# One-hots and spline products of a graph network on one core: the second operand of VectorE in PSUM

## What is computed

```python
h = relu(layernorm(x)); x = x + L0(h, edge_index, edge_attr_2)    # two SplineConv layers, 25 weights
h = relu(layernorm(x)); x = x + L1(h, edge_index)                 # normalised neighbour sum
h = relu(layernorm(x)); x = x + L2(h, src, dst, edge_attr_32)     # message MLP, sum, update MLP
h = relu(layernorm(x)); x = x + L3(h, src, dst, edge_attr_16)     # three message layers, batchnorm between

# a SplineConv layer
xw = einsum('ni,kio->nko', h, W)             # 25 products per node
g = xw[src[:, None], widx]                   # 4 of them per edge
msg = einsum('es,eso->eo', basis, g)         # weighted by 4 coefficients of the edge
out = segment_sum(msg, dst) / max(deg, 1) + h @ root + bias
```

## Time and profile before

| | us |
|---|---|
| median of three runs | 19,718.14 |
| lowest, highest | 19,655.34, 19,722.63 |
| profiled execution | 19,663.67 |
| its span, first to last instruction | 19,661.8 |
| POOL busy | 11,671.0 |
| PE, DVE, ACT busy | 8,407.5, 4,924.1, 1,228.1 |

### The profile page before, as it was taken

One profiled execution on the slowest core, in us unless ns is written; L12 is line 12 of the kernel. 1 busy time (PEld: TensorE's weight loads), 2 busy tenths in 40 slices (PEclk: granted clock), 3 DMA queues, 4 the chain that ended last, 5 costly groups with the idle time before them and its releaser, 6 DMA issues.

```text
span 19661.8 us, 145045 instructions
## 1 busy us (share of the span) xinstructions
PE 8407.5 (43%) x34014; PEld 7084.8 (36%) x34014; DVE 4924.1 (25%) x8122; ACT 1228.1 (6%) x2808; POOL 11671.0 (59%) x11663
## 2 busy tenths in 40 slices
PE   7655555444443333334444433333323333333333
PEld 4333334333333333334444433333323333233333
DVE  5334444333342111112333321111111111211111
ACT  3101111000000000001111100000000000000000
POOL 0366666577676666656555556566556665466665
PEclk9877777677775555556766755555555555555555
DMA  7545555333332111113333321111111111111111
GB/s 292 215 148 175 186 173 188 114 100 101 98 101 55 27 30 30 30 43 91 92 91 91 90 51 24 23 23 24 21 28 24 23 24 23 26 24 26 26 25 25
DMA packets 1013135, 1476.05 MB, mean 75 GB/s; under 512 B 546589, under 2 KB 704574, under 8 KB 987470
## 3 DMA queue, kind: packets, MB, share of 16 engines
q0 software_dynamic: 426240, 764.57, 15.9%
q1 hardware_dynamic: 586830, 710.77, 10.7%
HBM read 970.98 MB, written 503.39 MB: 75 GB/s over the span
## 4 chain that ended last, share of the span: by engine, by line
another core or an unknown queue 55%; PE 17%; issue 14%; DVE 6%; POOL 3%; DMA 2%; SPq 1%; ACT 1%; DVEq 1%; ACTq 0%; POOLq 0%
PE PS L769 10%; PE PS L689 4%; POOL BIG L612 3%; DVE OH L1356 1%; DVE BIG L1369 1%; PE PS L802 1%; DMA AG<-acc 1%; PE PS L698 1%; PE PS L763 1%; DVE BIG L1376 1%; DVE BIG L1195 0%; DVE BIG L1384 0%; PE PS L678 0%; ACT STG L971 0%
## 5 line engine op out<-in xcount | busy, mean ns | idle before, releaser
L769 PE MATMUL PS<-BIG,OH 128*128 128x64 f32 (+3 forms) x23310 | 5759.4, 428 | 4181.3 <-DVE OH L1356 1549.7
L612 POOL DMA_INDIRECT BIG<-t_mp,IDX x4995 | 4832.4, 967 | 3306.8 <-issue 1790.0
L769 PEld LDWEIGHTS PS<-BIG,OH 128*128 128x128 f32 x23310 | 5073.8, 295 | 4741.2 <-issue 2524.9
L612 POOL DMA_INDIRECT BIG<-t_cell,IDX x3330 | 3594.9, 1080 | 2504.7 <-issue 1814.5
L1356 DVE TENSOR_TENSOR OH<-REL,IOTA 128x640 f32<-128x640 f32 x2331 | 1899.8, 822 | 3262.8 <-remote 2640.3
L763 PE MATMUL PS<-STG,CARRY 128*128 128x64 f32 (+3 forms) x1554 | 552.2, 452 | 4690.2 <-ACT STG L971 2899.5
L612 POOL DMA_INDIRECT BIG<-t_p,IDX x1665 | 1623.2, 975 | 1167.2 <-issue 478.5
L612 POOL DMA_INDIRECT BIG<-t_gcn,IDX x1665 | 1619.3, 973 | 976.1 <-issue 559.1
L763 PEld LDWEIGHTS PS<-STG,CARRY 128*128 128x128 f32 x1554 | 344.0, 276 | 4877.8 <-ACT STG L971 2868.2
L1369 DVE TENSOR_TENSOR BIG<-BIG,COEF 128x1280 f32<-128x1280 f32 x666 | 990.4, 1487 | 553.6 <-DMA BIG<-t_cell,IDX 520.4
L802 PE MATMUL PS<-BIG 128*128 128x128 f32 x3330 | 584.8, 338 | 995.9 <-DVE BIG L1376 822.1
(11 more groups left out here) (148 smaller groups left out, 3336.0 us busy)
## 6 DMA issues: line engine op xcount, KB each, us to landing
t_cell<-BIG SPq DMA_DIRECT2D x198, 2048.0 KB, 6.3
BIG<-in_dst_row SPq DMA_DIRECT2D x333, 240.0 KB
BIG<-t_mp,IDX POOLq DMA_INDIRECT x4995
BIG<-t_cell,IDX POOLq DMA_INDIRECT x3330
BIG<-t_gcn,IDX POOLq DMA_INDIRECT x1665
BIG<-t_p,IDX POOLq DMA_INDIRECT x1665
BIG<-in_ef SPq DMA_DIRECT2D x333, 80.0 KB
BIG<-t_q SPq DMA_DIRECT2D x333, 48.0 KB
```

The source lines that it names most:

```text
L612: nc.gpsimd.indirect_dma_start(to[:, j, :], None, table, bass.IndirectOffsetOnAxis(ap=IDX[:, s // CHUNKS, at:at + 1], axis=0)).then_inc(ga ...
L769: last = nc.tensor.matmul(WIN[:, 0:out_w], OH[:, s % CHUNKS, j * P:(j + 1) * P], src[:, j, :], start=False, stop=(s % CHUNKS == CHUNKS - 1 ...
```

## The change

The numbers 0 to 127 (`PIOTA`) and the coefficients of three groups (`PCOEF`, 60 columns each) get PSUM bank 1. After the setup DVE copies `IOTA` there once. `CARRY` and the one-hots read `PIOTA` in place of `IOTA`, and the products read `PCOEF` in place of `COEF`. In a spline pass DVE copies a group's coefficients to PSUM one group ahead: in a group's first chunk, between the one-hots and the product, it waits for the next group's `COEF` and copies it. The first group's copy stands ahead of the loop. A product waits for `coef_copied` in place of `coef_in`, and SP, before it loads over a `COEF` buffer, for `coef_copied` in place of `prod_ready`. DVE's spline loop goes through `edged_units`. To free bank 1, four results move: hidden sums of the MLP pass to banks 2 and 3, `RF` to bank 6, `YB` to bank 4, and the first spline pass's turned blocks from bank 2 to 4.

```diff
-        HIDP = bank(1, CT * HID)
-        TB = {"n0": 2, "n1": 2, "n2": 2, "n3": 2, "n4": 5, "n5": 2, "n6": 2, "n7": 2}
-        RF = bank(1, NB * 2 * F)
+        PIOTA = bank(1, P)
+        PCOEF = [PS[:, 512 + P + gi * TILES * 4:512 + P + (gi + 1) * TILES * 4] for gi in range(UNIT)]
+        HIDP = bank(2, CT * HID)
+        TB = {"n0": 2, "n1": 4, "n2": 2, "n3": 2, "n4": 5, "n5": 2, "n6": 2, "n7": 2}
+        RF = bank(6, NB * 2 * F)
...
-        YB = bank(3, NB * F)
+        YB = bank(4, NB * F)
...
                             if kind == "spline":
-                                sp.wait_ge(prod_ready, CHUNKS * (gb + g))
+                                sp.wait_ge(coef_copied, gb + g)
                                 hold(sp)
...
+            link(v.tensor_copy(PIOTA, IOTA[:, :]))
...
                     if c == 0:
-                        v.tensor_scalar(CARRY[:, :], IOTA[:, :], DELTA[:, bass.ds(g, 1)], None, ALU.is_equal
+                        v.tensor_scalar(CARRY[:, :], PIOTA, DELTA[:, bass.ds(g, 1)], None, ALU.is_equal
                                         ).then_inc(carry_ready, 1)
                     v.tensor_tensor(OH[:, c, :].rearrange("p (j e) -> p j e", e=P),
                                     bc(REL[:, bass.ds(at * CT, CT)], shape),
-                                    IOTA[:, :].unsqueeze(1).to_broadcast(shape), ALU.is_equal).then_inc(oh_ready, 1)
+                                    PIOTA.unsqueeze(1).to_broadcast(shape), ALU.is_equal).then_inc(oh_ready, 1)
+
+                def copy_coefficients(gi, u):
+
+                    dve.wait_ge(coef_in[gi], 16 * (ub + u + 1))
+                    v.tensor_copy(PCOEF[gi], COEF[:, gi, :]).then_inc(coef_copied, 1)
 
                 def body(u, s, first, last):
                     one_hots(u, s)
                     if kind == "spline":
                         gi = s // CHUNKS
+                        if s % CHUNKS == 0 and not (last and gi == UNIT - 1):
+                            copy_coefficients((gi + 1) % UNIT, u if gi < UNIT - 1 else u + 1)
                         dve.wait_ge(gathered[s], 16 * CT * (ub + u + 1))
-                        dve.wait_ge(coef_in[gi], 16 * (ub + u + 1))
+                        dve.wait_ge(coef_copied, gb + u * UNIT + gi + 1)
                         g = slot(s, CELL_W, SUM0_W).rearrange("p j (a f) -> p j a f", f=F)
-                        w = COEF[:, gi, s % CHUNKS * CT * 4:(s % CHUNKS + 1) * CT * 4]
+                        w = PCOEF[gi][:, s % CHUNKS * CT * 4:(s % CHUNKS + 1) * CT * 4]
...
+                elif kind == "spline":
+                    copy_coefficients(0, 0)
+                    edged_units(dve, body, node)
```

More of the change, by code:

```diff
@@ L227, in gnn_program @@
         carry_ready, win_staged, sums_landed = sem("carry_ready"), sem("win_staged"), sem("sums_landed")
-        ea_copied = sem("ea_copied")
+        ea_copied, coef_copied = sem("ea_copied"), sem("coef_copied")
         gathered = [sem(f"gathered{s}") for s in range(SLOTS)]
@@ L709, in node_slot @@
                         products(sem(f"{ph}_rf_ps"), [HT[0:F + 1, :]], [RFW[n][:, :]], 2 * F,
-                                 lambda b: 512 + b * 2 * F)
+                                 lambda b: 6 * 512 + b * 2 * F)
                     if s == 4:
@@ L742, in node_slot @@
                         pe.wait_ge(sem("n4_u_ready"), k + 1)
-                        products(sem("n4_y_ps"), [UT[:, :]], [UW2[:, :]], F, lambda b: 3 * 512 + b * F)
+                        products(sem("n4_y_ps"), [UT[:, :]], [UW2[:, :]], F, lambda b: 4 * 512 + b * F)
                 if n >= 4:
```

## The result

The changed kernel takes 20,217.69 us (median of three runs, 20,215.97 to 20,220.55) against 19,718.14: 1.0266 of the kernel before, 95% interval 1.0237 to 1.0295. It is 500 us slower, above the range of the prediction (19,150 to 19,840), and the sign is the other one.

The account below looks back on a forecast made before the run. The prediction took POOL, busy 59% of the span with indirect transfers, as the bound. Savings of 45 us (spline passes) and 108 (other five) less 20 for copies gave -133 us: 19,585 against the 19,718.1 median, range 19,150 to 19,840.

Parts of the forecast that it names:

- What bounds the kernel: All seven passes: POOL, busy 59% of the span, sets the pace; its own work of 2,080 us is four fifths of a pass.
- Where transfers stretch: POOL's transfers wait for DVE instructions with two SBUF inputs: 453 us in the spline passes, 215 in the other five.
- Parts 1 and 2: One-hots (822 ns) and products (1,487 ns) with their second operand in PSUM: no change in time.
- Part 3: CARRY (777 of 291 ns) reading PSUM: taken as 0, with bounds of -12 and +52 us.
- Part 5: Added coefficient copies in the spline passes: 222, 48 us in all, 20 us on the path.
- Part 6: DVE's added wait for the next group's coefficients: nothing, with 2 us of margin; 240 us at worst.
- Parts 4 and 7: Results moved to other banks, and SP waiting for the copies in place of the products: nothing.
- Does POOL's gain reach the end?: Of POOL's saved time, 45 of 453 us stay in the spline passes and 108 of 215 in the other five.
- The reason behind it: Other engines hardly move while POOL runs unbroken; a product holding POOL for 1 us probably gives them a moment to go on.
- Worse: Rival, chance 0.18: starved phases grow, up to +150 us per spline pass; 19,930 us with both.
- Kept: Rival, chance 0.25: POOL sets the pace throughout and its idle pauses stay; -630 us, 19,088 at full.
- Nothing freed: Rival, chance 0.12 (including all given back): a broadcast PSUM operand holds POOL as SBUF does; transfers stay at 1,080 ns, 19,738 us.

Follow-up runs that it names:

- e5: The changed kernel, unedited, measured again: 15,938.25 us, 0.970 of the kernel before, which took 16,438.46 us in that session.
- e14: The changed kernel, unedited, measured again: 15,960.29 us, 0.970 of the kernel before, which took 16,456.25 us in that session.
- e11: The changed kernel with products, one-hots and CARRY reading SBUF again, copies and banks kept: 19,555.34 us, 0.998 of the kernel before (19,599.68 us in that session).
- e3: The changed kernel with products, one-hots and CARRY reading SBUF again, copies and banks kept: 16,451.59 us, 1.001 of the kernel before (16,435.89 us in that session).
- e9: The changed kernel with products, one-hots and CARRY reading SBUF again, copies and banks kept: 16,444.07 us, 1.001 of the kernel before (16,435.40 us in that session).
- e12: The changed kernel, unedited, measured again: 19,892.04 us, 1.012 of the kernel before, which took 19,651.37 us in that session.
- e4: The changed kernel plus a 512-column POOL memset ahead of each chunk in both spline passes: 16,481.33 us, 1.003 of the kernel before (16,435.89 us in that session).
- e15: The changed kernel plus a 512-column POOL memset ahead of each chunk in all seven passes: 18,373.00 us, 0.935 of the kernel before (19,657.86 us in that session).
- e16: The changed kernel, unedited, measured again: 20,236.54 us, 1.029 of the kernel before, which took 19,657.86 us in that session.

## Why the prediction was wrong

- **What bounds the kernel**: half right. POOL's own 2,080 us per pass are the floor, and prompt runs stand on it. In the late condition, from which the prediction was made, POOL's pace and its waiting are coupled, and neither can be changed alone.
- **Where transfers stretch**: right. The means came out at 949 and 946 to 952 ns and POOL's busy time at 11,050 (forecast: 947 and 945, near 11,020). The page "SBUF — State Buffer" of the Trainium skill, section "Who interferes with whom", says that tensor_tensor was not seen to stall transfers. Against it stand means of 1,080 and 1,079 ns with two SBUF inputs and 949 with one in PSUM.
- **Parts 1 and 2**: right, 816 and 1,481 ns. The fixed cost of the page "VectorE: DVE Perf Modes", section "The TRN2 errata", doesn't show in them. **Part 3**: I took 0; it is +57 ns, 45 us of DVE time, near the upper bound of 52. That is near the 65 ns which the prediction estimates from that page, but one size can't tell a fixed cost from a slower rate. Nothing of it is seen at the end: e5 and e14 have it and gain. **Part 5**: 48.4 us of copies, as worked out; 20 on the path was too much in the late condition, since e11 shows none; e3 and e9 are 16 and 9 us above before. **Part 6**: the product waited 2.0 us in all for a copy, and the copies 34.0 for their coefficients. **Parts 4 and 7**: as good as nothing, by the same three runs.
- **"Does POOL's gain reach the end?"**: this step failed. It let a tenth of 453 us and half of 215 stay, that is, it took the waiting to grow by less than what is saved, and so came to -133 us where +500 was measured. In fact the second spline pass lost 225 us of stretching (235 to 10) and gained 337 of waiting (284 to 621); the `t_gcn` pass lost 42 (47 to 5) and gained 101 (471 to 572). For one microsecond saved, 1.5 and 2.4 were waited (over the whole kernel 1.9, and some 1.4 by the smaller loss of e12). The sum of 519 and 518, which I read as a constant, is now 631 and 577. Two passes that agree at two working points fixed no law; the earlier trace rows had no third pass at another pace, and the t_mp pass (669, which the prediction works out itself) already spoke against a constant.
- **The reason behind it**: not borne out. The prediction has the other engines stand still while POOL runs, and a product's hold as a moment in which they move. That they hear late of each other in a late session is shown (9.65 us in the mean above). That holds or rests are their moments is not: in the second spline pass of before some 310 held transfers, with 1 us behind each, cover 29% of the time, and only 27% of ACT's restarts fall there, and with rests the share says nothing, as e4 and e15 show. What the runs show in its place is that less is waited the slower POOL goes; why, they don't.
- **The rival Worse** had the sign and, for the second spline pass, the size: over 2,700 (2,711), +112 of the +150 asked for. Its mechanism differed: not pauses of 13 to 15 us but three times as many of 8.3 us (589/71). It was under-sized because I let the other five passes keep 108 us, where they lost 282 (59, 122, 17, 23, 61). **Kept** is what happens when the session is prompt, -500 against its -630, though its condition, idle pauses that stay as they are, isn't met there: e3, which has the operands of before, has none. **Nothing freed** is refuted by the means.
- **The range** left out a give-back above one for the whole kernel. Its low end, 0.971 of before, would have needed a prompt session (0.970), of which no row of the late profile could tell.

What stays open: what puts a session in the late condition, by what path the other engines' messages are delayed there and why a slower POOL ends it, and why e12 lost 240 us where e16 lost 579. Rests between 0.74 and 1.06 us, or of another spacing, weren't tried.

## What to carry to other kernels

Before counting a faster engine as a gain, look whether its waiting is independent of its pace: here POOL's idle time followed a stretch in which others heard nothing, and each microsecond taken from the transfers cost 1.4 to 2.4 of waiting in the late condition. An engine busy for 55 to 59% of the span with hundreds of pauses of 5 to 13 us in the mean is not yet the bound. A deliberate rest of 1 us per five transfers shortened the whole by 6.5% in the late condition, and lengthened it by 11% in the prompt one. And measure the kernel before beside the changed one in every session, since the same change was worth -3.0% in one condition and +2.9% in the other.

## What the runs showed of the hardware

- With both inputs of DVE's products in SBUF the preparation of a `t_cell` transfer took 1,067 to 1,080 ns in the mean; with one input in PSUM, in products and one-hots, 946 to 949; in both conditions.
- A broadcast second operand in PSUM costs a tensor_tensor nothing (816 against 822 ns, 1,481 against 1,487). `CARRY`, a tensor_scalar over 128 columns, takes 348 ns from PSUM and 291 from SBUF.
- The same kernel takes 16,456 us in one session and 19,600 in another on the same chip; its sum passes have a granted clock of 0.50 in both conditions. In the late sessions, with a transfer every 1.25 us, ACT staged a window 9.5 us after PE's end in the mean and up to 43 us, in the prompt ones 0.13. In the pauses looked at, it took 5 to 7 us from POOL's stop to the first restart of another engine (5.0 above, 5.6 in the earlier trace rows, 7.0 in the earlier trace rows).
- At 1.46 us per transfer, with a break of over 1 us in every five, the lateness is gone in the second spline pass and the sum passes: 0.13 us, and 2,433 us for the second spline pass in either condition.
